# Two reorderings on VectorE in a fused gated-delta-rule and product-key-expert layer

## The reference

```
xn = layernorm(x)
x + attention(xn) + experts(xn)
```

```
q, k, v, z = split(xn @ w_qkvz);  b, a = split(xn @ w_ba)
q, k, v    = silu(causal_conv_4_taps(q, k, v))
beta, g    = sigmoid(b), -exp(A_log) * softplus(a + dt_bias)
q, k       = l2norm(q) * 128 ** -0.5, l2norm(k)
per token:  state = state * exp(g)
            delta = (v - state' k) * beta;  state += k delta';  o = state' q
y = rmsnorm(o * silu(z)) * norm_w;   attention = y @ w_out
```

```
h = silu(xn @ W_up' + b_up) @ W_down' + b_down
scores, indices = two-stage top-8 over product keys of h @ W_q'
z = silu((h . down_embed[indices]) * softmax(scores))
experts = sum over 8 heads x 8 experts of z * up_embed[indices]
```

## Time and profile before

| | |
|---|---|
| median of 3 runs | 3218.49 us (3217.93 to 3222.51) |
| the profiled execution | 3209.48 us |
| its span, first to last instruction | 3207.7 us |
| busy: PE, DVE, ACT, POOL | 91%, 92%, 56%, 69% of the span |
| mean granted TensorE clock | 0.975 of full speed |

### The profile page before, as it was taken

How to read it: one execution, slowest core, us unless ns; L and a number is a source line. 1 busy time by engine, 2 the same in 40 slices (tenths; PEclk the granted TensorE clock), 3 DMA queues, 4 the chain that set the end, 5 groups by cost and what they waited for, 6 DMA issues and landing times.

```text
span 3207.7 us, 56507 instructions
## 1 busy us (share of the span) xinstructions
PE 2926.0 (91%) x18444; PEld 2394.4 (75%) x18444; DVE 2951.7 (92%) x9293; ACT 1798.5 (56%) x4175; POOL 2218.9 (69%) x2394
## 2 busy tenths in 40 slices
PE   7942899999999999999999999999999999999997
PEld 4421678787878877878778877788787787877876
DVE  4997899999999999999999999999999999999996
ACT  3321555565556655565555655566555665656554
POOL 0003677877777777777777777787777777777764
PEclk9975999999999999999999999999999999999999
DMA  2002555555555555555555555555555565555653
GB/s 64 1 1 66 151 142 144 143 149 156 140 146 138 156 151 140 143 141 156 144 146 135 151 157 142 144 138 155 151 145 139 142 159 146 149 134 146 159 143 85
DMA packets 541829, 427.99 MB, mean 133 GB/s; under 512 B 247009, under 2 KB 450785, under 8 KB 541537
## 3 DMA queue, kind: packets, MB, share of 16 engines
q1 hardware_dynamic: 476000, 222.98, 25.6%
q0 software_dynamic: 65536, 201.39, 24.0%
HBM read 345.61 MB, written 45.09 MB: 122 GB/s over the span
## 4 chain that ended last, share of the span: by engine, by line
DVE 62%; PE 22%; ACT 8%; issue 5%; DMA 1%; POOL 1%; POOLq 1%; DVEq 0%; SPq 0%; ACTq 0%
DVE mix L1222 12%; DVE qkv L1181 9%; PE ps L584 4%; DVE E L1169 4%; DVE rows L1201 4%; PE ps L522 3%; DVE xg L1148 3%; PE ps L526 3%; PE ps L556 3%; PE ps L569 3%; PE ps L576 3%; DVE xr L1238 3%; ACT L824 2%; ACT L841 2%; DVE outer L1234 2%
## 5 line engine op out<-in xcount | busy, mean ns | idle before, releaser
L958 POOL DMA_INDIRECT rows<-table,idx_all x1024 | 1200.1, 1172 | 382.7 <-issue 280.3
L813 ACT ACTIVATE qkv<-qkv 128x512 f32<-128x512 f32 x256 | 161.4, 630 | 603.8 <-DVE qkv L1181 603.8
L942 POOL TENSOR_SCALAR xg<-xg,rms 128x128 f32<-128x128 f32 x520 | 407.3, 798 | 7.0
L576 PE MATMUL ps<-XT,E 128*128 128x128 f32 x3072 | 400.5, 277 | 0.0
L556 PEld LDWEIGHTS ps<-X,AT 128*128 128x128 f32 x3072 | 363.4, 192 | 35.7 <-DMA X<-whole 17.9
L1222 DVE SCALAR_TENSOR_TENSOR mix<-rows,zc,mix 128x256 f32<-128x256 f32 x896 | 381.3, 491 | 0.4 <-ACT zc L824 0.4
L556 PE MATMUL ps<-X,AT 128*128 128x128 f32 x3072 | 375.2, 275 | 3.3 <-DMA X<-whole 3.3
L576 PEld LDWEIGHTS ps<-XT,E 128*128 128x128 f32 x3072 | 368.7, 192 | 0.0
L946 POOL COPY gn<-gates 128x8 f32<-128x8 f32 x64 | 12.3, 193 | 481.3 <-SPq L330 262.2
L950 POOL TENSOR_SCALAR gm<-cst,gn 128x128 f32<-128x128 f32 x512 | 340.3, 680 | 6.5
L808 ACT ACTIVATE raw<-ps 128x512 f32<-128x512 f32 x256 | 152.9, 597 | 313.5 <-PE ps L522 313.5
(11 more groups left out here) (165 smaller groups left out, 6172.5 us busy)
## 6 DMA issues: line engine op xcount, KB each, us to landing
Wvz<-wvz SPq DMA_DIRECT2D x64, 512.0 KB, 3.2
xb<-xnT SPq DMA_DIRECT2D x64, 512.0 KB, 4.5
whole<-AT SPq DMA_DIRECT2D x128, 256.0 KB
X<-whole SPq DMA_DIRECT2D x128, 256.0 KB, 4.2
XT<-whole SPq DMA_DIRECT2D x128, 256.0 KB, 4.7
wo<-woh SPq DMA_DIRECT2D x65, 256.0 KB, 4.4
Wkq<-wkq SPq DMA_DIRECT2D x64, 256.0 KB, 2.9
rows<-table,idx_all POOLq DMA_INDIRECT x1024
```

The lines of the kernel that those rows point to most:

```text
L576: done = mm(ps[:, 4 + g, (a % 4) * P:(a % 4 + 1) * P], E[:, a, :], src[:, a, :], start=True, stop=True)
L942: pool.tensor_scalar(xg[:, a, :], xg[:, a, :], rms[:, a:a + 1], None, ALU.mult).then_inc(sm["y_p"], 1)
L958: pool.indirect_dma_start(rows[:, m, :], None, table[:, :], bass.IndirectOffsetOnAxis(ap=idx_all[:, f // 4, c:c + 1], axis=0)).then_inc(ga ...
```

## The change

It moves instructions on VectorE, and none is added or removed. First, `expert_mix` takes a range of rows. The first mix is cut in two: rows 0 and 1, then the three taps of k, then rows 2 and 3; `half_v` is raised behind rows 2 and 3, as before. Second, the four corrections of `RV` stand ahead of the three taps of the first value head instead of behind them.

```diff
-                def expert_mix(hf):
+                def expert_mix(k0, k1):
-                    dve.wait_ge(sm["silu_e"], at("silu_e", hf + 1))
-                    for k in range(hf * (K // 2), (hf + 1) * (K // 2)):
+                    dve.wait_ge(sm["silu_e"], at("silu_e", k0 // 4 + 1))
+                    for k in range(k0, k1):
...
                     level(0, 1)
-                    expert_mix(0)
+                    expert_mix(0, 2)
+                if front:
+                    for d in (1, 2, 3):
+                        tap(0, d)
+                if back:
+                    expert_mix(2, 4)
                     st.wait()
                     dve.sem_inc(sm["half_v"], 1)
-                if front:
-                    for d in (1, 2, 3):
-                        tap(0, d)
-                if back:
                     second_gated(nx)
...
-                    expert_mix(1)
+                    expert_mix(4, 8)
...
                     V.tensor_copy(xrT[:, :, :], rows_of(xr).rearrange("n i c -> n c i")).then_inc(sm["elim_v"], 1)
-                    for d in (1, 2, 3):
-                        tap(2, d)
                 if back:
                     dve.wait_ge(sm["ks_t"], at("ks_t", 1))
                     for b in range(2):
...
                             V.scalar_tensor_tensor(out=RV[:, a, :], in0=ps[:, 1, (2 * b + r) * P:(2 * b + r + 1) * P], scalar=neg_b[:, a:a + 1],
                                                    in1=RV[:, a, :], op0=ALU.mult, op1=ALU.add).then_inc(sm["r1_v"], 1)
+                if front:
+                    for d in (1, 2, 3):
+                        tap(2, d)
                 if front:
                     for d in (1, 2):
                         tap(3, d)
```

More of the change, by code:

```diff
@@ L1319, in one_pass @@
                     level(0, 1)
-                    expert_mix(0)
-                    st.wait()
-                    dve.sem_inc(sm["half_v"], 1)
+                    expert_mix(0, 2)
                 if front:
@@ L1326, in one_pass @@
                 if back:
+                    expert_mix(2, 4)
+                    st.wait()
+                    dve.sem_inc(sm["half_v"], 1)
                     second_gated(nx)
```

## The result

| | before | after |
|---|---|---|
| median | 3218.21 us (3212.65 to 3222.51) | 3299.94 us (3297.96 to 3303.2) |
| profiled execution, its span | 3209.48, 3207.7 us | 3297.96, 3296.1 us |
| mean granted TensorE clock | 0.975 | 0.962 |

The ratio is 1.0256 (1.0238 to 1.0274), 82 us more. The forecast was 3372 us.

What follows compares the result with a forecast made beforehand. Bound: a chain over VectorE, TensorE and ScalarE, neither TensorE nor VectorE alone. Profiled 3209.5 us, plus 117 for passes, minus 11 hidden, plus 50 for clock falls, plus 9 to the median: 3374, given as 3372; range 3292 to 3425 us.

Steps and rivals of the forecast that it cites:

- The late `half_v`: VectorE's first mix: signal behind three taps (2.3 us) and 0.1 us of waiting for ScalarE's copies, 2.4 us later.
- TensorE's wait before line 539: Wait for `silu(0)` goes, but the same 1.0 us is waited one step later for line 1272; worth nothing.
- GpSimd's delay: Gathers and scalings move 2.4 us later at unchanged length, delaying TensorE's state product by 1.46 us a pass.
- The room before the state product: TensorE's idle time for VectorE's line 1307, a cushion of 0.77 us, is used up by the later `projection(3)`.
- Case 4: GpSimd makes up its delay by short gathers or scalings; ScalarE's 0.4 us stay: 3244 us, chance 0.08.
- The rule of the Trainium skill: VectorE instructions with two SBUF inputs and GpSimd's SBUF reads exclude each other; scalings would shorten away from the mixes.
- ScalarE's list: In-order work at the pass's end: no idle time before `silu(3)`, next table load later by 0.4 us from order.
- VectorE's wait for `ks_t`: With the taps moved behind the `RV` corrections, VectorE waits another 1.45 us for `ks_t`.
- The falls: TensorE's clock drops in about half the passes, behind its wait before the last four transposes: 50 us.
- hidden ones: Today's irregular passes cost 14 us; about 11 us are hidden ahead of TensorE's wait for GpSimd.
- The signs of being wrong: `xg` scalings under 1.5 us later, TensorE waiting under 1 us for them, or the clock staying at full speed.
- The sum: Profiled 3209.5 + 117 - 11 + 50 = 3365.5 us; 9 us more for the median, 3374, rounded to 3372.

Runs made afterwards that it cites:

- e7: Kernel before, with `half_v` raised only when k's third tap is finished, order of work unchanged: 3370.92 us, ratio 1.0403.
- b2: Kernel before, unchanged, run again on the second chip; the kernel before took medians of 3235.08 to 3236.39 us there.
- a2: Kernel after, unchanged, run again on the second chip: 3530.58 us, ratio 1.0895 against the kernel before.
- part two alone: Kernel before with only the corrections of `RV` moved ahead of the first value head's taps, first mix and `half_v` as before: 3270.24 us, ratio 1.0108.
- e5: Kernel after plus one unused 128x512 matmul in TensorE's wait before `projection(1)`: 3546.7 us, ratio 1.095 against the kernel before.
- e6: Kernel before with k's taps between the mixes, plus one unused matmul in TensorE's wait before `projection(1)`: 3433.72 us, ratio 1.0622.
- e4: Kernel after, but `half_v` raised twice, behind rows 0 and 1 and behind rows 2 and 3: 3350.94 us, ratio 1.0348 against the kernel before.
- e8: Kernel after, but GpSimd does `finish` (scaling `xg`) ahead of the first eight gathers: 3382.85 us, ratio 1.0467 against the kernel before.
- e3: Kernel before with only `half_v` raised later, behind k's taps (waiting for the second tap): 3275.23 us, ratio 1.0117.
- e1: Kernel before with only k's taps moved between the rows of the first mix, `RV` corrections unmoved: 3419.74 us, ratio 1.0569.

## Why the prediction was right in sign and too high

**The late `half_v`: right.** Predicted 2.4 us later, measured 2.64. VectorE's wait for ScalarE's copies was 0.19 and not 0.1.

**TensorE's wait before line 539: right in its length, wrong in its worth.** It was to be "waited for one step later", about 1.0 us for line 1272. It is 1.13 us, and `projection(1)` starts 0.23 later. But I called the move worth nothing, and it brought the falls (below).

**GpSimd's delay: this step failed in its size.** I had let the gathers take what they took before, so that the last scaling ends 2.4 us late, with the shorter scalings as the only way out. The scalings stayed as long (6.61 for 6.37 us), and the gathers became 1.4 us shorter in this pass. The last scaling is late by 1.48, `projection(3)` likewise (1659.74 - 1634.09 = 25.65, against 24.17). The room before the state product then took its 0.94 as predicted, and 0.54 us are left where I had 1.46. Case 4 named gathers that could give time back and had chance 0.08; "nothing idle to give back" was my reason against it. The row that spoke for it was there: in the earlier trace rows the first gather takes 1.46 us, while the third (shown above) takes 0.95. That the later start is enough to shorten them is shown: in e7, with before's order on VectorE, the eight are busy for 8.2 us on average, against 9.5 in b2. Why is not. The first two of before lie beside k's taps, which those of after don't, but on average that is 0.5 of the 1.2 us; the last three of the eight give 0.8. The rule of the Trainium skill that I had weighed (SBUF — State Buffer, Who interferes with whom) was to shorten the scalings where VectorE has left the mixes. The kernel after didn't test it, since the second mix moved too and the scalings still lie beside it. The traces agree with the rule as far as they go: a scaling beside the mix takes 0.84 us on average and one beside the short elimination steps behind it 0.60, and in a2, whose second mix starts 3.4 us later than in b2, the eight take 5.3 us instead of 6.4.

**ScalarE's list: right in kind, smaller.** There is no idle time before `silu(3)`, and the table load is 0.76 us later, 0.22 more than the state product. I had 0.40. On the second chip part two alone moved the table load by 0.48, of which 0.10 were there at the state product.

**VectorE's wait for `ks_t`: right in kind, smaller.** Predicted 1.45 us, measured 1.00 in this pass and 53.3 / 64 = 0.83 on average, less because TensorE was less late.

**The falls: right number, wrong place.** I took half of the passes, and 33 of 63 have one. But they were to come behind the transposes' wait, and all sit in `projection(1)`, behind the shorter wait. e5 and e6 show why: with the wait filled, no fall is left there; and over both chips there are 17 to 44 in the kernels in which the wait follows the one-column products, and 0 to 13 where it stands ahead of them. The Trainium skill (TensorE: Matmul & The Clock Gate, Why this matters for your kernels) lists longer idle gaps than 1.1 us as the danger; by it there would be none. Both errors about the clock cancel, and that is luck: I had +50 for new falls and -11 for hidden ones, and it was 26 more falls x 1.5 = +39.

**The signs of being wrong.** One of them came up, by a hair: the scalings end 1.48 us later and not 1.5. The other is divided: TensorE waits 1.21 us for them in a pass without a fall, but 46 us in all, 0.7 a pass, where I had over 100, and its waits for line 1307 are not gone: they stand in the passes with a fall.

**The sum.** 1.86 us a pass became 0.76, 117 became 48 us. With the measured terms the sum for the profiled execution is 3209.5 + 48 + 39 = 3296.5; it took 3297.96. (My 3372 stands for 3374; that step was no rounding.)

**What stays open.** The profile of the first chip shows no late signals, and no part was run alone there: how its 82 us divide between the parts is read from the trace and not shown by a run. On the second chip the late signals go with most of a2's further loss: line 629 comes 1.9 us later than in the kernel after on the first chip, and the passes are 3.8 us longer on average (49.93 us against 46.16) with the falls that follow. Shown is that a later start of the gathers lengthens them, with little else changed (e7), and that an early start (e4) or a very late one (e8) takes the larger part away at this place. That it is the meeting of gathers with strip-wise transfers is a guess from where they lie; no run changed the strips, and the DMA share is the same on the chip that has no late signals. By what path a signal or a product of TensorE is delayed, and whether it is the chip that makes the difference, I can't say. The 1.0256 therefore holds for the chip that it was measured on.

## What to carry to other kernels

Before moving a signal, list everything that it starts, the transfers above all, and look at what those will then run beside: here a signal 1.4 to 2.2 us later, with the order of work untouched, cost 39 and 136 us on the second chip (e3, e7). Where a wait is expected to move "one step later" for nothing, look at what TensorE does just ahead of its new place. And when instructions of one kind have unequal durations in the profile (0.95 to 1.47 us here), don't carry their sum over to another place as a constant.

## What the runs showed of the hardware

- TensorE's clock fell to 1.2 GHz after a wait of only 1.1 us that stood right behind eight one-column products: 33 falls in 63 passes at this place, 7 with the wait ahead of these products; with a matmul in the wait none (44 in e1, 0 in e6). On the first chip a pass with a fall was 1.5 us longer in the median.
- An indirect gather's issue on GpSimd took 0.94 to 1.76 us; the mean went from 1172 to 1034 ns when the gathers started 2.6 us later.
- A scaling of 128x128 on GpSimd took 0.84 us on average beside VectorE's two-input mixes and 0.60 beside its small elimination steps (before and after).
- In the runs on the second chip, results of TensorE were seen by idle ScalarE and VectorE 2 to 4 us late (a2), and signals of no other compute engine were; on the first chip none was, at the same DMA share of about 0.85. The same change costs 2.6% on one and 9.0% on the other.
